# Graph attention in two layers: exponentials of layer 1 taken against the top of one eighth of the rows, and the last eighth prepared inside layer 1's first group

## The reference

```python
def layer0(h, W, a, adj):           # THR = 1e-4, ALPHA = 0.2
    h = h @ W
    e = leaky_relu((h @ a[:128])[:, None] + (h @ a[128:])[None, :], 0.2)
    valid = (adj > 0) & (h.sum(axis=1) != 0)[None, :]
    att = softmax(where(valid, e, -1e9), axis=1), 0 where not valid
    L = valid.sum(axis=1)
    att = where(att >= THR, att, 0) * L[:, None]      # 0 in rows whose top is <= THR
    return elu(h + att @ h)
def layer1(h, W, a, adj):
    Wh = h @ W
    e = leaky_relu((Wh @ a[:128])[:, None] + (Wh @ a[128:])[None, :], 0.2)
    return softmax(where(adj > 0, e, -9e15), axis=1) @ Wh
x = x + layer0(relu(layernorm(x)), W0, a0, adj)
x = x + layer1(relu(layernorm(x)), W1, a1, adj)
```

## Time and profile before

| what | value |
|---|---|
| median of 3 runs | 2001.0 us |
| the profiled execution, its own time | 2002.7 us |
| its span in the trace | 2000.9 us |
| busy: TensorE / VectorE / ScalarE / GpSimd | 96% / 87% / 73% / 63% |
| mean granted clock | 0.98 |
| one group of layer 0 / of layer 1 | 117.9 us / 114.85 us |
| last matmul of layer 0 to first of layer 1 | 1033.8 to 1065.9 us |
| mean DMA traffic | 284 GB/s |

### The profile page before, as it was taken

How to read it: one execution, slowest core, us unless ns; L and a number is a source line. 1 busy time by engine, 2 the same in 40 slices (tenths; PEclk the granted TensorE clock), 3 DMA queues, 4 the chain that set the end, 5 groups by cost and what they waited for, 6 DMA issues and landing times.

```text
span 2000.9 us, 39030 instructions
## 1 busy us (share of the span) xinstructions
PE 1914.1 (96%) x16858; PEld 1902.6 (95%) x16858; DVE 1750.4 (87%) x2026; ACT 1453.3 (73%) x1677; POOL 1255.5 (63%) x1010
## 2 busy tenths in 40 slices
PE   4789999999999999999968999999999999999997
PEld 3689999999999999999967999999999999999997
DVE  7888898989989898998957998898989899898985
ACT  4988788969888798888820767777777777778700
POOL 3675766767777676767720556767777776768600
PEclk9799999999999999999988999999999999999999
DMA  8998897999989898897982777888988888889900
GB/s 247 350 339 340 287 334 245 335 335 317 317 287 320 275 321 304 280 320 272 325 283 96 269 295 275 293 311 293 337 276 325 283 296 309 294 315 306 316 10 13
DMA packets 182339, 567.49 MB, mean 284 GB/s; under 512 B 18704, under 2 KB 50832, under 8 KB 180752
## 3 DMA queue, kind: packets, MB, share of 16 engines
q0 software_dynamic: 142848, 520.16, 74.4%
q1 hardware_dynamic: 34960, 42.67, 6.4%
q10 hardware_dynamic: 4352, 2.10, 0.5%
HBM read 548.54 MB, written 16.32 MB: 282 GB/s over the span
## 4 chain that ended last, share of the span: by engine, by line
PE 89%; DVE 6%; DMA 2%; ACT 1%; POOL 1%; issue 0%; SPq 0%; DVEq 0%; POOLq 0%
PE psum L659 87%; PE psum L632 1%; DMA arena<-in_adj_dram,piece_rows 1%; DVE arena L906 1%; DVE arena L740 1%; DVE arena L891 1%; ACT arena L343 1%; DVE arena L884 1%; PE psum L621 0%; DMA arena<-in_x_dram 0%; DVE st L715 0%; POOL piece_rows L379 0%; PE psum L599 0%; DVE arena L361 0%; DVE h_all L761 0%
## 5 line engine op out<-in xcount | busy, mean ns | idle before, releaser
L659 PE MATMUL psum<-h_all,arena 128*128 128x129 f32 x16384 | 1842.4, 276 | 10.4 <-DVE arena L906 10.4
L659 PEld LDWEIGHTS psum<-h_all,arena 128*128 128x128 f32 x16384 | 1837.9, 192 | 14.0 <-DVE arena L906 9.2
L333 POOL DMA_INDIRECT arena<-in_adj_dram,piece_rows x992 | 1246.1, 1256 | 641.4 <-ACT arena L343 446.1
L343 ACT ACTIVATE arena<-arena,half_step 128x1024 uint8<-128x1024 int32 x992 | 1365.1, 1437 | 313.1 <-DVE arena L361 161.3
L906 DVE SCALAR_TENSOR_TENSOR arena<-arena,rho_col 128x1024 f32<-128x1024 f32 x896 | 1125.8, 1277 | 169.1 <-PE psum L659 165.0
L361 DVE STREAM_TRANSPOSE arena<-arena 128x1024 f32<-128x1024 f32 x248 | 305.9, 1234 | 9.1 <-ACT arena L343 9.1
L906 DVE SCALAR_TENSOR_TENSOR arena<-psum,rho_col,arena 128x1024 f32<-128x1024 f32 x128 | 158.7, 1267 | 17.7 <-PE psum L659 14.6
L343 ACT ACTIVATION_READ_ACCUMULATOR arena<-arena,half_step 128x1 f32 x512 | 91.0, 178 | 0.0
L632 PE MATMUL psum<-W_ext,arena 128*128 128x131 f32 x256 | 40.5, 324 | 13.8 <-DVE h_all L761 10.7
L632 PEld LDWEIGHTS psum<-W_ext,arena 128*128 128x128 f32 x256 | 38.1, 234 | 15.4 <-issue 8.1
L621 PE MATMUL psum<-ident,arena 128*128 128x128 f32 x128 | 20.0, 308 | 32.9 <-DVE arena L740 32.5
(11 more groups left out here) (111 smaller groups left out, 180.9 us busy)
## 6 DMA issues: line engine op xcount, KB each, us to landing
arena<-in_adj_dram,piece_rows POOLq DMA_INDIRECT x992, 5.9
arena<-in_x_dram SPq DMA_DIRECT2D x48, 128.0 KB, 6.2
x_mid<-arena SPq DMA_DIRECT2D x8, 512.0 KB, 5.5
edgesT<-arena SPq DMA_DIRECT2D x4, 1024.0 KB, 8.9
arena<-edgesT SPq DMA_DIRECT2D x4, 1024.0 KB, 11.1
arena<-r_mid SPq DMA_DIRECT2D x1, 4096.0 KB, 12.0
arena<-x_mid SPq DMA_DIRECT2D x8, 512.0 KB, 6.8
out_dram<-arena SPq DMA_DIRECT2D x32, 128.0 KB, 9.8
```

What stands on the lines that cost most here:

```text
L333: pool.indirect_dma_start(adj_in[n % NA], None, adj_pieces, bass.IndirectOffsetOnAxis(ap=piece_rows[:, column:column + 1], axis=0))\
L343: nc.scalar.activation(pack_bytes[h][:, k, a], adj_in[n % NA], ACT.Sign, bias=half_step[:, 0:1], accum_out=into).then_inc(masked, 1)
L659: last = nc.tensor.matmul(acc_tile(g, k), wTs[m % RING][:, k * P:(k + 1) * P], h_all[:, j, 0:FZ], start=(j == 0 and k % 2 == 0), stop=(j = ...
```

## The change

Layer 1 no longer waits for the top of all d. Its exponentials are shifted by the top of the first eighth's d (`ref`), which is known in layer 0's third group; `top` and `low` of all rows are still found, later, and the verdict now also asks that `top - ref` is at most `REACH` = 20. r is taken as `exp(-0.8 (s + ref))`, limited from above by `R_LIMIT` where it was `max(s + top, 0)` before the exponential. ScalarE makes D, rho and r of each eighth right behind its product (`keep_sd`, `next_exps`), scales h by D as it copies it (eight copies of one tile where there were two of four tiles), and `fold` remains for the first eighth alone. The parts of h, the r rows of six groups and the kept edges are loaded within layer 0's last group, each behind a wait for the tile that frees its place. The last eighth (index 7) is finished, transposed, projected and scaled within layer 1's first group, whose last eight tiles need it; extremes, the mean and the verdict stand there too. Layer 1's first group reads r from `r_row` instead of PSUM.

```diff
+READY = NG - 2
+REACH = 20.0
+R_LIMIT = math.exp((1.0 - ALPHA) * REACH)
+        ref = base
+        D_next, rho_next, r_next = [sd_col[:].rearrange("p t k -> p (t k)")[:, i * T:(i + 1) * T] for i in range(3)]
...
-            r = r_ps if g == 0 else r_row[:, row * GW:(row + 1) * GW]
+            r = r_ps if layer == 0 and g == 0 else r_row[:, row * GW:(row + 1) * GW]
...
+            def load_h1(i):
+                if i == 0:
+                    sp.wait_ge(h1_stored, 16 * READY)
+                sp.wait_ge(summed, (NG - 1) * T + (i + 1) * TP)
+                sp.dma_start(h_all[:, part_of(1, i), 0:F], h1_mid[i].rearrange("p (t f) -> p t f", f=F))\
+                    .then_inc(first_loaded if i == 0 else h1_loaded, 16)
...
-            for g in range(1, NG):
+            for g in range(1, NG - 1):
                 store_x(g - 1)
                 load_xr(g)
                 store_h1(g - 1)
...
+            load_h1(0)
+            load_h1(1)
+            store_r(1, 0, READY * TP)
+            load_r(2, slice(0, READY * GW))
+            load_h1(2)
+            load_h1(3)
+            sp.wait_ge(edges_stored, 16 * SUBS)
+            load_kept(0)
+            store_x(NG - 2)
+            load_h1(4)
+            load_kept(1)
+            load_h1(5)
+            load_kept(2)
+            load_xr(NG - 1)
+            load_kept(3)
...
-            sp.wait_ge(edges_stored, 16 * SUBS)
-            for s in range(SUBS):
-                load_kept(s)
-            sp.wait_ge(h1_stored, 16 * (NG - 1))
-            sp.wait_ge(hr_ready, NG)
-            sp.wait_ge(summed, NG * T)
-            for i in range(NG - 1):
-                sp.dma_start(h_all[:, part_of(1, i), 0:F], h1_mid[i].rearrange("p (t f) -> p t f", f=F))\
-                    .then_inc(h1_loaded, 16)
             store_x(NG - 1)
-            store_r(1)
-            load_r(2, slice(0, N))
+            store_r(2, READY * TP, T)
+            load_r(3, slice(READY * GW, N))
             sp.wait_ge(x_stored, 16 * NG)
             sp.wait_ge(z_turned[1], NG)
...
+            def next_exps(t0, t1):
+                d, c = sd_next[:, t0:t1, 1], slice(t0, t1)
+                nc.scalar.activation(rho_next[:, c], d, ACT.Exp, scale=1.0 - ALPHA, bias=exp_bias[:, 1:2])
+                nc.scalar.activation(r_next[:, c], sd_next[:, t0:t1, 0], ACT.Exp, scale=ALPHA - 1.0, bias=exp_bias[:, 1:2])\
+                    .then_inc(next_ready, 1)
+            def keep_sd(i, half):
+                act.wait_ge(h_done[1], 2 * i + half + 1)
+                ps = h_ps(1, i, half)
+                nc.scalar.activation(sd_next[:, half_of(i, half), :], ps[:, :, F:F + 3], ACT.Identity)\
+                    .then_inc(sd_kept, 1)
+                if i >= 1:
+                    nc.scalar.activation(D_next[:, half_of(i, half)], ps[:, :, F + 1], ACT.Exp, scale=ALPHA,
+                                         bias=exp_bias[:, 0:1]).then_inc(D_next_ready, 1)
...
             def keep_h(i):
-                if i < NG - 1:
+                if i == 1:
+                    act.wait_ge(ref_ready, 1)
+                    act.wait_ge(sd_kept, 2)
+                    nc.scalar.activation(D_next[:, part_of(1, 0)], sd_next[:, part_of(1, 0), 1], ACT.Exp, scale=ALPHA,
+                                         bias=exp_bias[:, 0:1])
+                if i < READY:
                     act.wait_ge(x_stored, 16 * (i + 1))
                 for half in range(2):
...
-                    nc.scalar.activation(into, ps[:, :, 0:F], ACT.Identity).then_inc(h_kept[1], 1)
+                    keep_sd(i, half)
+                    if i == READY:
+                        act.wait_ge(summed, (NG - 1) * T + (READY + 1) * TP)
+                    act.wait_ge(D_next_ready, 2 * i + half - 1)
+                    for t in range(half * TP // 2, (half + 1) * TP // 2):
+                        b = i * TP + t
+                        into = tiles(ye)[:, t, :] if i < READY else h_all[:, b, 0:F]
+                        last = nc.scalar.activation(into, h_ps(1, i, half)[:, t - half * TP // 2, 0:F], ACT.Identity,
+                                                    scale=D_next[:, b:b + 1])
+                    last.then_inc(h_kept[1], 1)
+                act.wait_ge(sd_kept, 2 * (i + 1))
+                next_exps(0 if i == 1 else i * TP, (i + 1) * TP)
+            def set_D(t0, t1):
+                nc.scalar.activation(h_all[:, t0:t1, F:FZ], D_next[:, t0:t1].rearrange("p (t o) -> p t o", o=1),
+                                     ACT.Identity).then_inc(D_set, 1)
...
+            act.wait_ge(summed, (NG - 1) * T + (NG - 1) * TP)
+            set_D(0, (NG - 1) * TP)
             elu(NG - 1)
-            warm_up(2, ACT.Sqrt)
             deviation(1, NG - 1, part_of(1, NG - 1))
-            warm_up(3, ACT.Exp)
-            keep_zT(NG - 1)
-            keep_h(NG - 1)
-            exps(1)
             for n in range((NG * COLS + 1) * PIECES, len(PASSES) * PIECES):
+                if n == (NG * COLS + 1) * PIECES + 6:
+                    keep_zT(NG - 1)
+                if n == (NG * COLS + 1) * PIECES + 9:
+                    keep_h(NG - 1)
+                    set_D((NG - 1) * TP, T)
                 mask_piece(act, n)
...
+                    if layer == 1 and g == 0 and j == 0:
+                        pe.wait_ge(h1_loaded, 16 * (READY - 1))
+                        pe.wait_ge(h_folded, FOLDS + 1)
+                        pe.wait_ge(D_set, 1)
+                    if layer == 1 and g == 0 and j == (NG - 1) * TP:
+                        pe.wait_ge(h_kept[1], 2 * NG)
+                        pe.wait_ge(D_set, 2)
...
+                        if g == 2 and j == 16:
+                            turn_extremes(1)
+                        if g == 2 and j == 22:
+                            spread_extremes(1)
+                        if g == NG - 1 and j == 14:
+                            turn_r(1, spare_ps, 0, READY * TP)
...
+                    elif g == 0:
+                        if j == 26:
+                            turn_z(1, NG - 1)
+                        if j == 30:
+                            products(1, NG - 1)
+                        if j == 41:
+                            pe.wait_ge(h_kept[1], 2 * NG)
+                            pe.wait_ge(mean_ready, 1)
...
+                        if j == 49:
+                            turn_extremes(2)
+                            turn_r(2, rT_ps[:, P:2 * P], READY * TP, T)
+                        if j == 54:
+                            spread_extremes(2)
...
-            turn_z(1, NG - 1)
-            products(1, NG - 1)
-            spread(1)
...
+            def find_reference(step):
+                if step == 0:
+                    dve.wait_ge(sd_kept, 2)
+                    nc.vector.tensor_reduce(extremes[:, 0:1], sd_next[:, part_of(1, 0), 1], AX.X, ALU.max)\
+                        .then_inc(extremes_ready, 1)
...
+            def limit_r(no, t0, t1):
+                dve.wait_ge(next_ready, no)
+                nc.vector.tensor_scalar(r_next[:, t0:t1], r_next[:, t0:t1], R_LIMIT, None, ALU.min).then_inc(r_limited, 1)
...
                 else:
-                    link(nc.vector.tensor_tensor(flag[:, 2:3], flag[:, 2:3], flag[:, 1:2], ALU.max))
+                    link(nc.vector.tensor_tensor(verdict[:], verdict[:], flag[:, 2:3], ALU.max))
+                    link(nc.vector.tensor_tensor(flag[:, 2:3], top[:], ref[:], ALU.subtract))
+                    link(nc.vector.tensor_scalar(flag[:, 2:3], flag[:, 2:3], REACH, None, ALU.is_gt))
                     link(nc.vector.tensor_tensor(verdict[:], verdict[:], flag[:, 2:3], ALU.max))
...
+            last_at = {5: 0, 7: 1, 9: 2, 12: 3, 13: 4, 14: 5, 20: 6, 21: 7, 22: 8}
+            reference_at = {12: 0, 19: 1, 26: 2}
...
+                    if g == NG - 1 and j == 11:
+                        limit_r(READY - 1, 0, READY * TP)
+                    if g == NG - 1 and j == 18:
+                        keep_rows(1, spare_ps, READY * TP)
+                    if g == NG - 1 and j == 40:
+                        fold_first_part()
...
-            for step in range(9):
-                finish_0(NG - 1, step)
-            extreme_values(1)
-            diagonals(1)
-            dve.wait_ge(exps_ready, 2)
-            dve.wait_ge(h1_loaded, 16 * (NG - 1))
-            dve.wait_ge(h_kept[1], 2 * NG)
-            fold(1, 0)
-            dve.wait_ge(r_spread, 2)
+            dve.wait_ge(r_loaded[2], 16)
+            dve.wait_ge(next_ready, NG - 2)
             for g in range(NG):
...
+                    if g == 0 and j in last_at:
+                        finish_0(NG - 1, last_at[j])
+                    if g == 0 and j == 36:
...
+                    if g == 0 and j == 40:
+                        limit_r(NG - 1, READY * TP, T)
+                    if g == 0 and j == 46:
...
+                        highest_and_lowest(sd_next[:, :, 1]).then_inc(extremes_ready, 1)
+                    if g == 0 and j == 53:
```

(9 more changed lines are left out.)

201 lines of the change are left out of this document (115 added, 86 removed).

## The result

| | before | changed |
|---|---|---|
| median | 2000.3 us (4 runs, 1998.11 to 2002.02) | 1983.64 us (4 runs) |
| the profiled execution, its own time | 2002.7 us | 1985.87 us |
| its span in the trace | 2000.9 us | 1984.1 us |

The ratio is 0.9912, with a 95% interval of 0.9895 to 0.993; that is 17.6 us of 2000.3, where I forecast 26 and 1975.0 us. One of the four executions took 2205.01 us at a granted clock of 0.848; the ratio leaves it out, the median of 1983.64 includes it, and the other three have a median of 1981.41. The time lies at the upper end of the range, 1969.5 to 1984, and outside the forecast's own band, a gain of 23 to 29.

What follows compares the result with a forecast made beforehand. TensorE was taken to set the pace, VectorE following. Gain 27.6 us at the seam, less 1.0 for layer 0's additions and 0.7 for DMA, about 26: from 2001.0 to 1975.0 us, range 1969.5 to 1984.

Steps and rivals of the forecast that it cites:

- The seam: Layer 0's last matmul to layer 1's second group, fifth tile: 156.4 us before, 128.8 forecast, a gain of 27.6.
- VectorE's two stalls: Layer 1's start: VectorE's extra work stalls TensorE 1.8 us in the first group, 0.2 + 1.4 at the second's start.
- lead of 4.0 us: With the ring of four tiles full, VectorE is ahead of TensorE by about 4.0 us, which absorbs extra work.
- Layer 0's small additions: Extra transposes and a small product on TensorE in layer 0's third and last groups: 1.0 us, bounds 0.3 and 1.2.
- ScalarE: `keep_h` some 3.5 us longer, ELU 1.3 shorter; hidden by waits, taken as 0, bound 1.5.
- The seam's loads: Kept edges and rows needed at layer 1's start land in time, hidden, with 3 us or more to spare.
- The two DMA due points: Layer 0's last group: added loads delay pieces for turn 15 and `keep_zT(6)`; 0.7 us together, bounds 0 and 6.
- signs of being wrong: TensorE stalling at tile 38 or tile 53's products, VectorE waiting at the seam, or idle time at tile 30's products.
- rival (b): Layer 0's last group: row load takes half the DMA engines; gain 17 to 21 us, 1980 to 1984; chance 0.16.
- (a): VectorE's stalls absent or half as long and DMA free: gain 29 to 31 us, 1970 to 1972; chance 0.12.
- (c): Layer 1's first group: chained work late by a queue's length, TensorE waits; gain 8 to 17 us; chance 0.07.
- (d): The verdict's `REACH` test fails and both layers run the general program, 6.5 ms or more; chance 0.02.

Runs made afterwards that it cites:

- best: Changed kernel with five r-row blocks, h parts 3 to 5 and the verdict's last steps later, the last eighth's steps mostly earlier: 1968.38 us, ratio 0.9858.
- again: The changed kernel measured once more without an edit: 1985.82 us, ratio 0.9937 to the kernel before.
- rows: Changed kernel, with only the first group's r rows loaded in layer 0's last group and the other 2.6 MB in layer 1: 1974.64 us, ratio 0.9883.
- other_bytes: rows_harts with five 512 KB loads of unneeded h data put in place of the five moved row blocks: 1981.75 us in one run.
- rows_harts: Changed kernel with five of six r-row blocks loaded in layer 1 and h parts 3 to 5 behind the last kept-edge load: 1973.69 us, ratio 0.9874.
- split_rows: Changed kernel with h parts 3 to 5 loaded later and the 3.1 MB of r rows as six 512 KB loads: 1977.93 us in one run.
- seam: Changed kernel with the last eighth finished, transposed, projected and scaled between the layers again: 2002.76 us in one run.
- harts_kept: Changed kernel with h parts 3 to 5 and the kept-edge loads moved later, the r-row load left whole: 1987.18 us.

## Why the prediction was right and wrong

- **The seam, right.** 128.1 us against 128.8. There is no gap and the granted clock is 1.00. The last eighth's work has the prices of the earlier trace rows inside the group.
- **VectorE's two stalls, right in place, too large in size.** I put 1.8 at tiles 20 to 26 and 0.2 + 1.4 at tile 4 of the second group. The brackets show 0.17, 0.17 and 0.21 at tiles 22, 23 and 26, and 0.96. A bracket understates: from 1084.99 to 1087.21 a tile takes 2.22 us, not 1.79. By the stretch of `best`, 125.9 with only the usual 0.23, they cost 2.2 beyond it, where I had 3.2. My lead of 4.0 us and forms of 1.22 were a little too dear.
- **Layer 0's small additions**, forecast 1.0: the counts come 1.4 us later, 1.2 of it behind the start-up (137.63 against 137.50). Right.
- **ScalarE**: `keep_h(5)` takes 4.7 us from first to last where it took 1.5, 3.2 more against 3.5 forecast. The table load of `keep_h(1)` lies in its wait for the products, as said.
- **The seam's loads, right.** VectorE waits neither for `edgesT` nor for the rows, and TensorE doesn't wait at the products of tile 30.
- **The two DMA due points: here the prediction failed.** "I take 0.7 us for both points, bounds 0 and 6" measured about 10, beyond its bounds. The stall at the products of tile 53 was among my signs of being wrong, and it came. That the time still lies in the range is the room that rival (b) gave it, not this term. Three steps of it:
  - The start of the row load. I had the 24 KB store land in some 3 us; it landed in 11.1, as it stood behind an h part. The load left at 957.55 and missed turn 15, whose last mask was on time, and met the masks ahead of the deviation and of turn 16.
  - A due point that I didn't count. `deviation` stands on ScalarE behind masks of pieces, at tile 44. I had asked only for turn 15 and `keep_zT(6)`. VectorE waited 4.7 us for it, more than its lead, and TensorE lost 1.8 us between counts and transposes (9.83 by the earlier trace rows, 11.66 now).
  - The 11 us to spare at `keep_zT(6)`. They were not enough: ScalarE came to the conversion at 1022.71, where it had been ready at 1002.03 (1007.00 less its wait of 4.97), 20.7 us later. I had worked from the bytes that don't fit, 4 to 15 us late, which reaches past the 11, and still took the near end. The 340 to 387 GB/s in that working stood in none of my rows; over 930 to 1002 the engines then moved 369. To the 6.54 of waiting I added no clock: the products themselves ran 1.5 longer.
- **Rival (b)**, the row load taking half the engines, is the nearest to what came: 17 to 21 us of gain forecast, 17.6 measured by the ratio, 12.6 in `again`. Its mechanism, that pieces wait behind a row load, holds by `rows` and `other_bytes`, and so does its half rate: in the 13.3 us of the row load the pieces moved 2.04 MB at a share of 0.39, against 4.15 MB at 0.91 before. Its due points were wrong: the 3 us at turn 15 didn't come, and up to 4 us at the other point stand against 8.0 measured (6.54 and the 1.5 of clock) and 1.8 at the deviation. That its sum fits is luck. The Trainium skill ("DMA: Bandwidth & Descriptors", Queues, rings and completion order) has the engines go round between queue rows by packets. The trace agrees with that as far as it goes: the load had a share of 0.59 beside the pieces' 0.39. But the larger of TensorE's two waits, 6.54 us, goes with one issue of 9.09 us, about which that rule says nothing.
- Rivals (a), (c) and (d) didn't come: DMA cost about 10 us, nothing was late by a queue's length in layer 1, and no general program ran.

**What stays open.** Why one issue of GpSimd takes 3.1, 4.3, 5.5, 6.7, 8.1 or 9.1 us. It stands at nearly the same place in each kernel, the 538th to 542nd of 992 issues, and it exists at 3.11 in the kernel before. Its length fell when the rows were moved or cut (`rows`, the `rows_harts` kernels, `split_rows`) and rose again with `other_bytes`, but it stayed at 9.09 when only h parts or kept edges were moved, and `seam`, where no load was touched, has 8.10. In `harts_kept` it was 9.09 when the loads had landed 14 us and more before. No run here shows what the issue waits for. Nor do the runs separate the two parts of the loss cleanly: a kernel with the long issue and without late pieces wasn't built.
